# Keys of four batch pairs, then the values: reordering the projection stage of a cross-attention and dequantised-FFN kernel

## The chip, the core and the metric

The kernel runs on one core of a Trainium2 chip. The metric is the device time of one execution in microseconds (us); below, "time" means that. The engines are TensorE (PE: products and transposes; its weight loads are listed as PEld), VectorE (DVE), ScalarE (ACT), GpSimd (POOL) and SyncE (SP), whose queue issues nearly all DMAs. The engines run side by side and are held in order by semaphores alone; each executes its own list strictly in order.

## The reference

```python
# x, ctx: (8, 256, 1024) float32; 32 query heads, 8 key/value heads, head size 128
h = layernorm(x)
q = rope((h @ wq) by heads);  k = rope((ctx @ wk) by heads);  v = (ctx @ wv) by heads
x = x + softmax(q @ k.T / sqrt(128) + mask) @ v @ wo
# FFN: the row norm of a layer-normed row of 1024 is about 32, under the threshold of 64,
# so only the 4-bit table is ever picked
w = take_along_axis(lut4, the 4-bit codes of qweight)      # (1024, 1024), by bit planes
x = x + layernorm(x) @ w.T + bias
```

Every operand of a product is a float32 number split in a high part (rounded to fp32r) and a low part (the rest), and every product is made of three passes: high by high, high by low, low by high.

## The kernel before

The work has three stages. The **projection stage** makes the keys and values of all batches, writes them (high and low) to scratch memory, decodes the FFN weight, and prepares nine of the sixteen 128-row tiles of the first layer norm. The **attention stage** runs 256 units (head by batch) of queries, scores, softmax, values and output projection. The **FFN stage** is 16 row tiles by 1024 columns. The change is in the projection stage.

The projection stage goes over the batches in order (`batch(b)`, written out once for each engine). A batch has 8 key groups and 4 value groups. A key group `g` is 24 products on PE (8 chunks of the contraction by three passes, L846), with 128 columns of `wk` as the stationary operand and the 256 context columns of one batch as the moving one. Its result lies in half a PSUM bank; `k_ps` has two such places. Then ACT swaps the halves of the head into `rope_x` or `probs` (L1028, L1029), DVE multiplies the product by the cosine table (`rope_cos`, L1409), the swapped copy is multiplied by the sine table (`rope_sin`: DVE at L1418, in batch 0 POOL at L1987), DVE adds (L1424), ACT rounds to the high part (L1033), DVE subtracts for the low part (L1428) and SP stores (L581). PE may start group n when the cosine product of group n-2 is done, since that frees its bank. A value group is 24 products with 512 columns of `wv` moving (L823) into `wide_ps`; ACT rounds it, DVE subtracts (L1586), SP stores.

The context of one batch (transposed, split) lives in `ctxT`, 4096 columns of `R`. The next batch's split (ACT L1037, DVE L1433) waits until the last value group has used a chunk. `wk` fills `W` and `wv` fills `X`, split once in batch 0 (`piece_hi`, `piece_lo`, L1104 and L1544).

A layer-norm tile is loaded as rows; ACT makes mean, centre, squares and root, DVE the factor, ACT scales the row (L1069). Then PE transposes it (`turn_row`, L784, 8 products) and ACT and DVE split it (`x_high` L1082, `x_low` L1459). The seven tiles that are left for the attention stage take another way: the same statistics from rows, but the data is loaded a second time as columns (`load_columns`), the two factors come back through memory as a broadcast row, DVE adds and multiplies (L1466, L1470), ACT rounds, DVE subtracts (L1474), and nothing runs on PE.

The decoding of the FFN weight is 8 tiles of 17 DVE operations (`decode`): bit planes spread (8 small instructions, L1600), a flip (L1608), 8 leaves (L1619, 128x1024 int32) and 7 picks (L1626, COPY_PREDICATED). ACT widens bit 0 (`full_bit0`, L1162). PE transposes each decoded tile (`turn_weights`, L804) and ACT and DVE split it (L1152, L1586).

Of the kernel before, what the change touches and what calls it, by code (L numbers as in the profile page):

```python
# [14 lines left out]
def build_xattn_ffn(nc, x, ctx, mask, wq, wk, wv, wo, qweight, lut4, bias, x_rows, x_columns, rope_cos, rope_sin, out):  # L15
# [5 lines left out]
    ALU, ACT = mybir.AluOpType, mybir.ActivationFunctionType  # L21
# [23 lines left out]
    A_ROPES = NB * HKV  # L45
# [8 lines left out]
    A_TURNS = 2  # L54


    V0, V1, V2, V3, D0, D1 = range(6)
    STAGED = 6
    K_TURNS = {V1: 4, V3: 5}
    V_TURNS = {V0: 0, V2: 1, D0: 2, D1: 3}  # L60
    K_SLOT0 = HKV // 2 + len(K_TURNS)
# [3 lines left out]
    WARM = 24  # L65
    FIRST_LOADS = ((8, 9), (10,), (11, 12), (13,), (14, 15))
    FIRST_PIECES = ((3,), (4,), (5,), (6,), (7,), (8,), (9, 10), (11,))


    CARRY = {1: ((12, 13), (14,), (15,), (16,)), 2: ((15,), (16,))}  # L70
    OWN = {1: {4: 0, 5: 1, 6: 2, 7: 3}, 2: {2: 0, 3: 1, 4: 2, 5: 3, 6: 4, 7: 5}}
    LAST_OP = {0: 11, 1: 14}
    CTX_AT = {1: (2, 4), 2: (4, 7)}
# [80 lines left out]
    K_ROW = {1: 0, 2: 1, 3: 3, 4: 5, 5: 7, 6: 8}  # L154
    V_ROW = {2: 2, 3: 4, 4: 6}
    TURN_AT = [None, 5, 3] + [1] * (NB - 4)
    SECOND_AT = [None, 7, 6] + [4] * (NB - 4)
    A_ROWS = len(K_ROW) + len(V_ROW)
# [3 lines left out]
    PE_TILES = A_ROWS  # L162
# [22 lines left out]
    with ExitStack() as stack:  # L185
# [11 lines left out]
        wk_s = W[:, :].rearrange("p (c l n) -> p c l n", c=C, l=2)  # L197
        wv_s = X[:, :].rearrange("p (c l n) -> p c l n", c=C, l=2)
        ctxT = R[:, 0:4096].rearrange("p (c l n) -> p c l n", c=C, l=2)
        k_stage = R[:, 4608:5632].rearrange("p (s l n) -> p s l n", s=2, l=2)  # L200
        k_stage_all, v_stage_all = R[:, 4608:5632], R[:, 5632:6656]
# [3 lines left out]
        xT = X[:, :].rearrange("p (c l n) -> p c l n", c=C, l=2)  # L205
# [14 lines left out]
        ctx_stage = acc_t[:, 0:2048].rearrange("p (c n) -> p c n", c=C)  # L220
# [17 lines left out]
        a_raw = [raw, ln_row[:, :]] + [acc[:, t, :] for t in range(2, HT)]  # L238
        rope_x = sb("rope_x", [P, 2 * S], F32)
        rope_a = sb("rope_a", [P, 2 * S], F32)  # L240

        ropes = [(rope_x[:, 0:S], rope_a[:, 0:S]), tuple(prob_t[:, i * S:(i + 1) * S] for i in range(2))]
# [19 lines left out]
        k_ps = [bank[3][:, 0:S], bank[4][:, 0:S]]  # L262
# [10 lines left out]
        ctx_in = [sem(f"ctx_in{t}") for t in range(TS)]  # L273
# [8 lines left out]
        first_hi, first_lo = sem("first_hi"), sem("first_lo")  # L282
# [6 lines left out]
        v_stored, d_stored, first_stored = sem("v_stored"), sem("d_stored"), sem("first_stored")  # L289
        x_stored, res_stored, out_stored = sem("x_stored"), sem("res_stored"), sem("out_stored")  # L290
# [6 lines left out]
        ctx_used = sem("ctx_used")  # L297
        stage_hi, stage_lo = sem("stage_hi"), sem("stage_lo")
# [20 lines left out]
        row_ok, x_tr, x_hi, x_lo = sem("row_ok"), sem("x_tr"), sem("x_hi"), sem("x_lo")  # L319
# [4 lines left out]
        def staging(b, i):  # L324

            if b == 0 and i == D0:
                return x_split_all, first_stored
            if b == NB - 1 and i == D0:
                return prob_t[:, :].bitcast(F32R), d_stored
            keys = (V1, D1) if b == NB - 1 else (V1, V3, D1) if b == NB - 2 and i == D1 else (V1, V3)  # L330
            return (k_stage_all, k_stored[0]) if i in keys else (v_stage_all, v_stored)

        def staged_count(b, i):
            if b == NB - 1:
                return b * STAGED + (V0, V1, V2, D0, D1, V3).index(i) + 1
            return b * STAGED + i + 1

        def v_turn(b, i):

            if b == 0:  # L340
                return {V0: 0, V2: 1, D1: 2}[i]
            return b * len(V_TURNS) - 1 + V_TURNS[i]

# [24 lines left out]

        def cols_tile(e):

            return ln_row[:, :].rearrange("p (c n) -> p c n", c=C)
# [47 lines left out]
        def early_output(h):  # L419

            return (acc[:, 2, :], picks[3], picks[2], picks[1])[h]

        def a_piece(k):

            if k < HKV:
                return wk_s[:, :, :, k * DK:(k + 1) * DK]
            c, n = 2 * (k % 4), (k - HKV) // 4
            return wv_s[:, c:c + 2, :, n * BANK:(n + 1) * BANK]

        def a_source(k):  # L430
            return a_raw[k % A_SLOTS].rearrange("p (c n) -> p c n", c=C if k < HKV else 2)
# [5 lines left out]
        def _(sp):  # L437
# [10 lines left out]
            def load_row(e):  # L448

                sp.wait_ge(x_tr, 2 * min(e, PE_TILES))  # L450
                if e > PE_TILES:
                    sp.wait_ge(lo_stored, 16 * (e - PE_TILES))
                sp.dma_start(ln_row[:, :], x_tiles[e]).then_inc(row_in, 16)
# [6 lines left out]
            def load_columns(e):  # L460

                sp.wait_ge(row_step, 4 * e + 4)
                sp.dma_start(cols_tile(e), x_columns[e]).then_inc(cols_in, 16)
                sp.wait_ge(factors_out, 16 * (e - PE_TILES + 1))
                sp.wait_ge(cols_step, 2 * (e - PE_TILES))
# [7 lines left out]
            def store_high(e):  # L473

                sp.wait_ge(cols_hi, e - PE_TILES + 1)
                sp.dma_start(column_parts(e)[HI], raw.rearrange("p (c n) -> p c n", c=C)).then_inc(hi_stored, 16)
# [1600 lines left out]
```

## Time and profile before

| | |
|---|---|
| time, median of 3 runs | 2337.54 us (2337.25 to 2340.97) |
| time of the profiled execution | 2336.49 us |
| its span, first to last instruction | 2334.7 us |
| TensorE clock granted | 1.00 of full speed |
| busy: PE / DVE / ACT / POOL | 2320.7 / 1703.8 / 1108.0 / 566.1 us |
| projection stage, first key product to first query product | 7.48 to 382.76 us |
| attention stage and FFN stage | from 382.76 us, and from 2156.56 us, to the end |

The profile is one execution. A busy engine is not an engine at its peak: PE is busy 99% of the span, so a shorter time needs either less work on PE or less waiting there. Idle time of the other engines costs nothing by itself.

### The profile page before, as it was taken

What the parts mean: (1) busy time and instruction counts of PE and PEld (TensorE: products, weight loads), DVE (VectorE), ACT (ScalarE), POOL (GpSimd) and SP (SyncE); (2) the same over time, 40 slices, a digit from 0 to 9 for tenths busy, and PEclk for the clock granted to TensorE, in tenths of its full rate; (3) what the DMA queues carried; (4) which work ended last, traced back from release to release, by engine and by line L of the source; (5) the groups of instructions that cost most, each with busy time, mean ns of one, the idle gap of its engine ahead of it and who ended that gap; (6) DMA issues with size and microseconds to landing.
All of it is one profiled execution on the core that took longest, in us unless ns stands there. A gap on an engine that the chain in (4) does not pass through costs nothing.

```text
span 2334.7 us, 35083 instructions
## 1 busy us (share of the span) xinstructions
PE 2320.7 (99%) x11846; PEld 1983.3 (85%) x11846; DVE 1703.8 (73%) x3818; ACT 1108.0 (47%) x2458; POOL 566.1 (24%) x675
## 2 busy tenths in 40 slices
PE   9999999999999999999999999999999999999999
PEld 8999999888888888888888888888888888888887
DVE  8888777677777777777776777677777777777763
ACT  6555544646454646455544445444544444444110
POOL 1000001323322233223222333232223232321321
PEclk9999999999999999999999999999999999999999
DMA  7466559545454544444556643343333333334442
GB/s 268 151 205 210 191 176 313 147 135 137 126 131 118 124 135 122 127 123 135 127 163 199 205 143 109 91 118 101 116 91 113 108 100 109 98 106 163 153 135 81
DMA packets 332898, 332.85 MB, mean 143 GB/s; under 512 B 33456, under 2 KB 268080, under 8 KB 332720
## 3 DMA queue, kind: packets, MB, share of 16 engines
q1 hardware_dynamic: 297296, 314.48, 44.8%
q10 hardware_dynamic: 35424, 16.14, 2.7%
q8 instruction: 95, 1.56, 0.3%
q14 instruction: 83, 0.68, 0.1%
HBM read 186.32 MB, written 71.31 MB: 110 GB/s over the span
## 4 chain that ended last, share of the span: by engine, by line
PE 95%; DMA 2%; DVE 1%; SPq 1%; ACT 0%; issue 0%; POOL 0%; ACTq 0%; DVEq 0%
PE bank L887 29%; PE bank L959 28%; PE bank L846 8%; PE bank L997 7%; PE bank L930 7%; PE bank L903 7%; PE bank L823 7%; DMA small_split<-probs 1%; SPq L666 0%; PE bank L784 0%; PE bank L804 0%; DMA ln_row<-in_L_xattn_wk 0%; DVE residual L1861 0%; DMA small_split<-k_scratch 0%; POOL probs L2001 0%
## 5 line engine op out<-in xcount | busy, mean ns | idle before, releaser
L887 PE MATMUL bank<-acts_split,weights_split 128*128 128x512 f32 (+1 forms) x3192 | 743.0, 382 | 0.0
L959 PE MATMUL bank<-weights_split,small_split 128*128 128x512 f32 x3072 | 739.4, 389 | 3.0 <-DVE small_split L1845 1.7
L959 PEld LDWEIGHTS bank<-weights_split,small_split 128*128 128x128 f32 x3072 | 575.3, 188 | 123.4 <-DVE small_split L1845 2.9
L887 PEld LDWEIGHTS bank<-acts_split,weights_split 128*128 128x128 f32 x3192 | 576.5, 188 | 109.6
L2001 POOL TENSOR_SCALAR probs<-probs,row_numbers 128x256 f32<-128x256 f32 x512 | 355.6, 706 | 1196.7 <-DVE row_numbers L1831 1196.7
L1297 ACT ACTIVATE probs<-bank,row_numbers 128x256 f32<-128x256 f32 x512 | 237.4, 470 | 129.4 <-DVE row_numbers L1826 129.4
L1835 DVE STREAM_TRANSPOSE probs<-probs 128x512 f32<-128x512 f32 x250 | 177.6, 710 | 142.3 <-POOL probs L2001 142.3
L1993 POOL TENSOR_TENSOR rope_x<-rope_x,sin_t 128x512 f32<-128x512 f32 (+1 forms) x133 | 166.8, 1254 | 396.3 <-ACT rope_x L1270 396.3
L1840 DVE TENSOR_TENSOR small_split<-small_split 128x512 fp32r<-128x512 f32 x250 | 178.6, 714 | 94.5 <-ACT small_split L1310 94.4
L1820 DVE CUSTOM_DVE_ANT_0 bank<-bank,mask_tile 128x256 f32<-128x256 f32 x512 | 207.2, 446 | 49.3 <-PE bank L903 49.0
L903 PEld LDWEIGHTS bank<-small_split 128*128 128x128 f32 x1536 | 217.5, 190 | 21.9 <-DMA small_split<-k_scratch 1.9
L903 PE MATMUL bank<-small_split 128*128 128x256 f32 x1536 | 224.4, 282 | 0.9 <-DMA small_split<-k_scratch 0.9
L1310 ACT ACTIVATE small_split<-small_split 128x512 fp32r<-128x512 f32 x250 | 157.8, 631 | 137.3 <-DMA small_split<-probs 137.1
L1323 ACT ACTIVATE small_split<-bank 128x512 fp32r<-128x512 f32 x127 | 75.8, 597 | 303.9 <-PE bank L930 303.9
L930 PE MATMUL bank<-small_split 128*128 128x512 f32 x762 | 197.6, 394 | 3.7 <-issue 2.0
L846 PE MATMUL bank<-small_split,weights_split 128*128 128x256 f32 x1536 | 187.7, 284 | 1.3 <-issue 0.8
L846 PEld LDWEIGHTS bank<-small_split,weights_split 128*128 128x128 f32 x1536 | 185.5, 192 | 2.2 <-issue 1.2
L823 PE MATMUL bank<-acts_split,small_split 128*128 128x512 f32 x768 | 178.1, 391 | 0.1
L997 PE MATMUL bank<-weights_split,acts_split 128*128 128x512 f32 x768 | 174.5, 389 | 0.0
L997 PEld LDWEIGHTS bank<-weights_split,acts_split 128*128 128x128 f32 x768 | 144.1, 188 | 29.9
L823 PEld LDWEIGHTS bank<-acts_split,small_split 128*128 128x128 f32 x768 | 143.0, 188 | 29.5 <-DVE acts_split L1544 0.5
L1861 DVE TENSOR_TENSOR residual<-residual,bank 128x512 f32<-128x512 f32 x256 | 163.7, 681 | 0.0
(126 smaller groups left out, 2159.6 us busy)
## 6 DMA issues: line engine op xcount, KB each, us to landing
small_split<-probs SPq DMA_DIRECT2D x754, 64.0 KB, 2.2
raw<-in_L_xattn_wq SPq DMA_DIRECT2D x61, 512.0 KB, 3.7
raw<-in_L_xattn_wo SPq DMA_DIRECT2D x60, 512.0 KB, 3.9
k_scratch<-small_split SPq DMA_DIRECT2D x64, 256.0 KB, 2.4
v_scratch<-small_split SPq DMA_DIRECT2D x32, 512.0 KB, 2.9
acts_split<-x_scratch SPq DMA_DIRECT2D x32, 512.0 KB, 5.7
mask_tile<-in_mask_BxSxS_ff SPq DMA_DIRECT2D x64, 256.0 KB, 2.9
small_split<-k_scratch SPq DMA_DIRECT2D x64, 256.0 KB, 3.0
```

What stands on the lines that cost most here:

```text
L823: done = pe.matmul(wide_ps[t][:, :], ctxT[:, c, a, t * P:(t + 1) * P], wv_s[:, c, m, n * BANK:(n + 1) * BANK], start=c == 0 and k == 0, st ...
L846: done = pe.matmul(k_ps[g % 2], wk_s[:, c, a, g * DK:(g + 1) * DK], ctxT[:, c, m, :], start=c == 0 and i == 0, stop=c == C - 1 and i == 2)
L887: last = pe.matmul(query_bank(j)[:, 0:wide], wq_s[:, h, c, a, :], xT[:, c, m, b * S:b * S + wide], start=c == 0 and i == 0, stop=c == C - ...
L903: last = pe.matmul(s_ps[:, t * S:(t + 1) * S], q_s[:, Q_SLOT[u], a, t * P:(t + 1) * P], k_s[:, m, :], start=i == 0, stop=i == 2)
L930: last = pe.matmul(o_ps[:, :], v_s[:, k, a, :], pT_keys[:, m, k], start=k == 0 and i == 0, stop=k == TS - 1 and i == 2)
L959: last = pe.matmul(out_ps[part][:, :], o_s[:, a, u % 2 * S + t * P:u % 2 * S + (t + 1) * P], wo_s[:, h, m, n * BANK:(n + 1) * BANK], start ...
L997: last = pe.matmul(out_ps[f % 2 * NN + n][:, :], xT[:, c, a, f % HT * P:(f % HT + 1) * P], w4_s[:, c, m, n * BANK:(n + 1) * BANK], start=c ...
L1297: last = act.activation(row, scored, ACT.Exp, bias=neg_max[:, u % 2, t:t + 1], accum_out=row_sum[:, u % 2, t:t + 1])
L1820: last = dve.tensor_tensor_reduce(out=s_ps[:, t * S:(t + 1) * S], in0=s_ps[:, t * S:(t + 1) * S], in1=mask_t[:, t, :], scale=1.0, scalar=- ...
L1835: dve.transpose(prob_rows[:, u % 2, :], prob_rows[:, u % 2, :]).then_inc(p_blocks, 1)
L1840: dve.tensor_tensor(pT_s[:, LO, u % 2, :], source, pT_s[:, HI, u % 2, :].bitcast(F32), ALU.subtract).then_inc(pT_lo, 1)
L2001: done = pool.tensor_scalar(row, row, row_inv[:, u % 2, t:t + 1], 1.0, ALU.mult, ALU.mult)
```

## The change

- **Keys.** All key groups come first, two batches in one product: 32 groups of 24 products with 512 moving columns (`keys(j)`), each filling a whole PSUM bank. All steps of the rotation are 512 wide. The sine product is always on POOL. `ropes[1]` takes the places of `probs` and `mask_tile`.
- **Values.** Then all 32 value groups, in four segments of 8. The batch pairs come in the order 3, 0, 1, 2, so pair 3 is still in place and the others are loaded and split a second time.
- **Layout.** The split context of a pair lies in a half of `X` or `W` (8192 columns). `wv` is split at steps 24 to 31 into halves that the keys have freed. In the values part the low split of the context is on POOL.
- **Norm tiles.** The nine tiles go through columns like the other seven: `turn_row`, `x_high`, `x_low` and `row_norm` go; `load_columns`, `load_factors`, `columns_center`, `columns_scale`, `columns_high`, `columns_low`, `store_high`, `store_low` come, at fixed steps.
- **Decoding.** The order of the 136 operations is a list `DECODE`, filled step by step from a budget. Context pieces and all other side work are put at fixed steps too.
- **Start.** The first two context pieces and the first `wk` piece are split in halves; four context pieces of 512 KB are loaded for the first pair; `WARM` goes from 24 to 30.
- The attention and FFN stages keep their order; only places in `X` differ.

```diff
-    A_ROPES = NB * HKV
+    A_ROPES = NB // 2 * HKV
...
+    V_GROUPS = NB * TS * NN
+    A_STEPS = A_ROPES + V_GROUPS
+    SEGMENT = 2 * TS * NN
+    V_PAIRS = (3, 0, 1, 2)
+    CTX_PAIRS = (0, 1, 2, 3) + V_PAIRS[1:]
+    CTX_HEAD = 4
+    CTX_STEP = (3, 4, 5, 6, 10, 11, 12, 13, 18, 19, 20, 21,
+                33, 34, 35, 36, 41, 42, 43, 44, 49, 50, 51, 52)
+    PIECE_STEP = (0, 1, 2, 3, 4, 24, 25, 26, 27, 28, 29, 30, 31)
+    ROW_BASE = tuple(3 + 6 * e for e in range(9))
...
+    for step in range(5, A_STEPS):
+        spent = min(spent, 150) + 520 - (215 if step < A_ROPES else 70)
+        spent -= 125 * ((step in CTX_AT and step < A_ROPES) + (step in SPLIT_AT) + (step in QUERY_AT))
+        spent -= sum(125 for base in ROW_BASE if step in (base + 2, base + 5, base + 6, base + 7))
+        spent -= sum(150 for end in ENDED.values() if step == end + 2)
+        DECODE[step] = []
+        while n < NB * TREE and spent > 0:
+            tile, op = n // TREE, n % TREE
+            DECODE[step].append((tile, op))
+            spent -= 120 if op == 0 else 16 if op == 1 else 128 if op in (4, 7, 8, 11, 14, 15, 16) else 77
...
+    TURN_AT = {end + 2: tile for tile, end in ENDED.items()}
...
+            def keys(j):
+                pair, g = j // HKV, j % HKV
+                if j == 0:
+                    pe.wait_ge(first_lo, 3)
+                elif pair == 0:
+                    pe.wait_ge(w_lo, g + 1)
+                pe.wait_ge(rope_cosd, j + 1)
+                for c in range(C):
...
+                    for i, (a, m) in enumerate(PASSES):
+                        done = pe.matmul(k_ps[j % 2][:, :], wk_s[:, g, c, a, :], ctx_slots[pair][:, c, m, :],
+                                         start=c == 0 and i == 0, stop=c == C - 1 and i == 2)
+                done.then_inc(rope_mm, 1)
+
+            def values(v):
+                segment, b, t, n = group(v)
+                if v % SEGMENT == 0:
+                    pe.wait_ge(ctx_lo, 4 * (segment + 4))
+                if v >= 2:
+                    pe.wait_ge(val_lo, v - 1)
...
+            for step in range(A_STEPS):
+                if step < A_ROPES:
+                    keys(step)
+                else:
+                    values(step - A_ROPES)
+                if step in TURN_AT:
+                    turn_weights(TURN_AT[step])
...
+            for step in range(A_STEPS):            # VectorE
+                if step < A_ROPES:
+                    rope_cos(step)
+                ops = DECODE.get(step, ())
+                if step < A_ROPES:
+                    for tile, op in ops[:1]:
+                        decode(tile, op)
+                    ops = ops[1:]
+                    rope_add(step, step % 2)
+                else:
+                    values_low(step - A_ROPES)
...
+                for tile, op in ops:
+                    decode(tile, op)
...
+                if step < A_ROPES:
+                    rope_low(step)
...
+            for step in range(A_STEPS):            # GpSimd
+                if step < A_ROPES:
+                    turned = fold(ropes[step % 2][0], (0, 1))
+                    pool.wait_ge(rope_in, 2 + step + 1)
+                    pool.tensor_tensor(turned, turned, table(sin_t, (0, 1)), ALU.mult).then_inc(rope_sind, 1)
+                if step in CTX_AT and step >= A_ROPES:
+                    q = CTX_AT[step]
+                    pool.wait_ge(ctx_hi, q + 1)
+                    pool.tensor_tensor(ctx_piece(q)[:, :, LO, :], ctx_stage[ctx_place(q)],
+                                       ctx_piece(q)[:, :, HI, :].bitcast(F32), ALU.subtract).then_inc(ctx_lo, 1)
```

The comments "VectorE" and "GpSimd" are added here. A "step" below is one pass of this loop, 0 to 63: one group on PE and the side work that belongs to it.

## Rows read from the trace of the kernel before

**Rows 1.** The page: its head line, and busy time by engine.
```profile
span 2334.7 us, 35083 instructions
...
PE 2320.7 (99%) x11846; PEld 1983.3 (85%) x11846; DVE 1703.8 (73%) x3818; ACT 1108.0 (47%) x2458; POOL 566.1 (24%) x675
```

**Rows 2.** Groups by line and form on PE: count, busy us, mean ns, idle before.
```profile
L846 PE MATMUL bank<-small_split,weights_split 128*128 128x256 f32 x1536 | 187.7, 284 | 1.3 <-issue 0.8 <-DVE weights_split L1544 0.5
L823 PE MATMUL bank<-acts_split,small_split 128*128 128x512 f32 x768 | 178.1, 391 | 0.1
...
L784 PE MATMUL bank<-ident,ln_row 128*128 128x128 f32 x72 | 9.3, 272 | 0.0
```

**Rows 3.** The chain that ended last: start us, length us, engine and line.
```profile
77.81 5.47 PE bank L823 x24
84.15 16.34 PE bank L823 x72
100.49 11.51 PE bank L846 x96
112.88 11.51 PE bank L846 x96
...
382.76 10.88 PE bank L887 x48
```

**Rows 4.** Timeline of the start: start us, length us, engine, line, what.
```profile
6.03 1.15 ACT L1108 ACTIVATE weights_split<-raw 128x512 fp32r<-128x512 f32 x2 [1.02 <-DMA raw<-in_L_xattn_wk]
...
7.48 3.36 PE L846 MATMUL bank<-small_split,weights_split 128*128 128x256 f32 x24 [0.82 <-issue]
7.67 1.15 ACT L1037 ACTIVATE small_split<-residual 128x512 fp32r<-128x512 f32 x2 [0.50 <-DMA residual<-in_ctx]
...
10.27 1.06 ACT L1104 ACTIVATE weights_split<-residual 128x1024 fp32r<-128x1024 f32 x1 [0.27 <-DMA residual<-in_L_xattn_wk]
...
11.30 20.42 PE L846 MATMUL bank<-small_split,weights_split 128*128 128x256 f32 x168 [0.46 <-DVE weights_split L1544]
```

**Rows 5.** Timeline, DVE and POOL side by side, in three places.
```profile
15.38 0.74 POOL L1987 TENSOR_TENSOR probs<-probs,sin_t 128x256 f32<-128x256 f32 x1 [2.20 <-ACT probs L1029]
...
15.78 0.63 DVE L1428 TENSOR_TENSOR small_split<-rope_a,small_split 128x256 fp32r<-128x256 f32 x1
...
445.16 1.21 DVE L1551 TENSOR_TENSOR weights_split<-raw,weights_split 128x1024 fp32r<-128x1024 f32 x1
445.34 1.83 POOL L2001 TENSOR_SCALAR probs<-probs,row_numbers 128x256 f32<-128x256 f32 x2 [7.68 <-DVE row_numbers L1831]
...
465.25 0.93 POOL L2001 TENSOR_SCALAR probs<-probs,row_numbers 128x256 f32<-128x256 f32 x2 [3.80 <-DVE row_numbers L1831]
```

**Rows 6.** Groups by line and form on DVE, 0 to 383 us.
```profile
L1626 DVE COPY_PREDICATED residual<-residual 128x1024 f32<-128x1024 uint8 x56 | 75.4, 1346 | 0.7
L1619 DVE TENSOR_SCALAR residual<-residual,probs 128x1024 int32<-128x1024 int32 x64 | 50.8, 818 | 1.1 <-ACT residual L1162 1.1
...
L1428 DVE TENSOR_TENSOR small_split<-probs,small_split 128x256 fp32r<-128x256 f32 x32 | 14.2, 442 | 0.1
```

**Rows 7.** Groups by line and form on POOL, whole span.
```profile
L1993 POOL TENSOR_TENSOR rope_x<-rope_x,sin_t 128x512 f32<-128x512 f32 x123 | 159.4, 1296 | 395.4 <-ACT rope_x L1270 395.4
L2015 POOL TENSOR_TENSOR residual<-residual,probs 128x1024 f32<-128x1024 f32 x16 | 38.3, 2399 | 112.6 <-DVE ln_row L1516 101.0 <-DMA probs<-in_L_ffn_bias 11.6
```

**Rows 8.** Groups by line and form on DVE, 383 to 2150 us.
```profile
L1796 DVE TENSOR_TENSOR rope_a<-rope_a,rope_x 128x512 f32<-128x512 f32 x123 | 85.1, 692 | 34.3 <-POOL rope_x L1993 31.5
```

**Rows 9.** Timeline, a stretch of decoding on DVE.
```profile
344.60 1.54 DVE L1619 TENSOR_SCALAR residual<-residual,probs 128x1024 int32<-128x1024 int32 x2 [1.05 <-ACT residual L1162]
...
346.17 1.32 DVE L1626 COPY_PREDICATED residual<-residual 128x1024 f32<-128x1024 uint8 x1
...
347.39 0.80 DVE L1619 TENSOR_SCALAR residual<-residual,probs 128x1024 int32<-128x1024 int32 x1
```

**Rows 10.** Groups by line and form on ACT, 0 to 383 us.
```profile
L1162 ACT ACTIVATE residual<-residual 128x1024 int32<-128x1024 uint8 x8 | 8.4, 1051 | 5.0 <-DVE probs L1608 3.1 <-DVE residual L1600 1.8
```

More of the change, by code:

```diff
@@ L261, in build_xattn_ffn @@
         w4_ps = [bank[0], bank[1]]
-        k_ps = [bank[3][:, 0:S], bank[4][:, 0:S]]
+        k_ps = [bank[3], bank[4]]
         q_ps = [bank[3], bank[4]]
@@ new lines, in _ @@
+            for tick in range(2, A_STEPS + 1):
+                if 0 <= tick - 2 < A_ROPES:
+                    store_keys(tick - 2)
+                if tick in CTX_AT:
+                    load_context(CTX_AT[tick])
+                if tick in ROW_STEP:
+                    if tick == ROW_BASE[0]:
+                        sp.wait_ge(ctx_lo, CTX_HEAD)
+                    load_row(ROW_STEP[tick])
+                if tick + 1 in SPLIT_AT and SPLIT_AT[tick + 1] >= HKV:
+                    load_split(SPLIT_AT[tick + 1])
+                for tile in range(1, NB):
+                    if tick == BEGUN[tile - 1] + 2:
+                        load_planes(tile)
+                    if tick == LUT_FREE[tile - 1] + 2:
+                        load_lut(tile)
+                if tick == A_STEPS - 10:
+                    sp.wait_ge(ctx_lo, 4 * len(CTX_PAIRS))
@@ new lines, in _ @@
+                if tick > A_ROPES:
+                    store_values(tick - A_ROPES - 1)
+                if tick - 3 in ROW_STEP:
+                    store_factors(ROW_STEP[tick - 3])
+                    load_columns(ROW_STEP[tick - 3])
+                if tick - 4 in ROW_STEP:
+                    load_factors(ROW_STEP[tick - 4])
+                if tick - 8 in ROW_STEP:
+                    store_high(ROW_STEP[tick - 8])
+                    store_low(ROW_STEP[tick - 8])
+                if tick - 1 in TURN_AT:
+                    for i in range(2):
+                        store_weights(TURN_AT[tick - 1], i)
@@ new lines, in values @@
+            def values(v):
[4 more added lines that the diff above has]
+                    pe.wait_ge(val_lo, v - 1)
+                first = b % 2 * S + t * P
+                for c in range(C):
+                    if v in (0, SEGMENT // 2) and c % 2 == 0:
+                        pe.wait_ge(w_lo, HKV + n * 4 + c // 2 + 1)
+                    for i, (a, m) in enumerate(PASSES):
+                        done = pe.matmul(wide_ps[v % 2][:, :], v_ctx[segment][:, c, a, first:first + P], wv_s[n][:, c, m, :],
+                                         start=c == 0 and i == 0, stop=c == C - 1 and i == 2)
+                done.then_inc(wide_mm, 1)
@@ L1303, in turned_high @@
                 act.wait_ge(o_mm, 1 + u // 2)
+                if u == 1:
+                    for s in range(2):
+                        act.wait_ge(v_stored[s], 16 + 8 * V_GROUPS)
                 if u in PE_TURNS:
@@ L1633, in decode @@
             def decode(tile, op):
-                A, B, C_, D_ = range(4)
+                A, B, C_, D_ = roles(tile)
                 if op == 0:
```

918 lines of the change are left out of this document (341 added, 577 removed).

## The prediction

> **What bounds the kernel now.** I read the page first: PE is busy 2320.7 of 2334.7 us [rows 1], so the end moves only if PE has less to do or waits more. Next the groups on PE: the key groups of the projection stage (L846) waited 1.3 us in all, the value groups 0.1 us [rows 2]. Then the chain of waits for lengths from start to start: a value group is 5.47 us for 24 products, a key group 11.51 / 4 = 2.88 us for 24 products of half the width [rows 3]. A busy mean of one product is no price, since products overlap. From the first key product (7.48 us) to the first query product (382.76 us) PE hardly ever stops [rows 3, 4]. So the change must be read in this stage, first as PE work, then as whether the helpers, mostly DVE, still keep up.
>
> The sum is made against the profiled execution, 2336.49 us (span 2334.7, some 1.8 us around it). That is 1.05 us under the median of the runs; I add that at the end.
>
> **Keys, two batches per product.** 64 groups of 2.88 us (184.3) go. 32 groups of 512 columns come. The trace has no such key group, but the value groups have the same form, 24 products of 128x512, at 5.47 us, and 48 query products take 10.88, the same to 1% [rows 3]: 32 x 5.47 = 175.0. Saving 9.3 us. Bounds: at the query price 32 x 5.44 = 174.1; if two narrow groups were no slower than a wide one, nothing.
>
> The Trainium skill ("TensorE: Matmul & The Clock Gate", Back-to-back issue gap) puts a lone warm product at N / 2.4 ns plus 2.5 ns, by which the 24 narrow ones would take 2.62 us and the wide ones 5.18, and the merge would save 1.9 us and not 9.3. The rows, 2.88 and 5.47, disagree with it for products that alternate with weight loads, so the rows decide.
>
> **Row tiles off PE.** Between two value groups lies a transposed tile: 84.15 - 77.81 - 5.47 = 0.87 us [rows 3]. There are 72 / 8 = 9 [rows 2]: 7.8 us go. Nothing is put in their place on PE. The weight turns stay: 112.88 - 100.49 - 11.51 = 0.88 each [rows 3], eight of them.
>
> **Start.** Before, the first key product began at 7.48; the second group began at 11.30, so the stage ran as if begun at 11.30 - 2.88 = 8.42 [rows 4]. The first pair needs the first and third transfers as context, the second as `wk`. They arrived so that ACT began at 6.03 (second) and 7.67 (third) [rows 4]. With halves (ACT 0.6, DVE 0.7 each) the third's first half is done at about 9.0, and keys start there, 1.5 us later than before. Chunks 4 to 7 need the fourth and fifth transfers; ACT began on the fifth at 10.27 [rows 4]. Behind six ACT halves and two whole pieces, DVE ends the last at about 13.0, while PE would be there at 9.0 + 2.7 = 11.8. So the first group ends near 15.7, as if begun at 10.3. Cost +1.9 us. The six extra warming transposes lie in the wait for the loads, so cost nothing; without that cover they are 6 x 0.2.
>
> **PE alone.** The stage would end at 10.3 + 64 x 5.47 + 8 x 0.88 = 367.4 in place of 382.76: **-15.4 us**, execution 2321.1.
>
> **Do the helpers keep up?** This is where I expect the gain to shrink. I price DVE from start to start, since its instructions overlap by some 0.1 us: 0.6 for 512 wide (0.69 long [rows 8]), 1.13 for 1024 two-source (1.21 long [rows 5]), 1.57 for two leaves (346.17 - 344.60), 1.22 for a pick (347.39 - 346.17), up to 1.35 where a pick follows a pick [rows 6, 9].
>
> POOL's part grows. Before, it had 8 sine products of 256 wide and was then idle until the queries. Now it has 32 of 512 at 1.29 us and 12 low splits of 1024; the nearest row of that shape takes 2.40 us [rows 7]. Does this cost DVE anything? The timeline says yes. While POOL multiplied from 15.38 to 16.12, DVE's two-source subtraction of 15.78 took 0.63, and 0.44 is its mean [rows 5, 6]. At 445.34 POOL's pair took 1.83, against 0.93 when alone at 465.25, and ended 0.80 after DVE's two-source instruction (to 446.37) did [rows 5]. That is one after the other, released about 0.14 before the end of each record. So a POOL instruction keeps a two-source DVE instruction out for its length less 0.14: 1.15 and 2.26 us. Sources in PSUM (cosine product, value and weight lows) go through.
>
> The Trainium skill ("SBUF — State Buffer", Who interferes with whom) says the same of two-source instructions and adds one-source instructions in a two-port mode, the leaves by their speed. The trace agrees for the former; no row shows the decoding beside POOL.
>
> Sums over steps, by the `DECODE` list:
> - Steps 5 to 31: rotation 27 x 1.8 = 48.6, decoding 35.1, context splits 11.3, `wv` splits 9.0, norm tiles 4.7 + 13.6 (twelve column operations), weight lows 2.4. DVE 124.6, POOL 27 x 1.15 = 31.0, together 155.6. PE has 27 x 5.47 + 2 x 0.88 = 149.4. Excess 6.2.
> - Steps 32 to 60: decoding 94.3, value lows 17.4, columns 16.9, the rest 10.9. DVE 139.5, POOL 27.1, together 166.6, against PE's 163.0. Excess 3.6. Besides, ACT waits for DVE's bit planes in order to widen bit 0, 1.05 us [rows 10], and rounds the next value group (0.58) only behind that. With DVE late it then has nothing to do for 1.6 to 1.8 us, in five tiles: +9.
>
> Total excess 18.8. Off it: PE needs a bank again one step later, so DVE may lag by 5.47 - 0.62 - 0.69 = 4.2 us before PE notices; and in the quarter of the key steps in which DVE isn't late, the cosine product lies beside POOL's instruction, 7 x 0.6 = 4. What reaches PE: 18.8 - 4.2 - 4 = **10.6 us**. Bounds: nothing, if the decoding isn't kept out (then DVE has 124.6 for 149.4 and 139.5 for 163.0); and 19, if neither credit holds.
>
> **Other parts.** ACT loses 18 half-tile roundings and 9 scalings and gains 9 roundings of columns and 12 context pieces; its steps come to at most 6.3 us and about 2.8 on average, so it has room. Column loads, factor stores and broadcasts (3 to 5 us to land) are issued by SP one to three steps ahead; behind SP's wait for the factor (L457) stands the next key store, which is not due before that either. The second loading of 12 context pieces adds 6 MB to a stage that moves 80. The first query needs its `wq` split, made from step 60 on, and context and turned rows, loaded from tick 56 on, 4 to 8 steps ahead. All this I cost at nothing; a load that comes a step late costs up to 5 us once. The other stages have the same work and order: 0.
>
> **Sum.** 2336.5 - 15.4 + 10.6 = 2331.7 on the profiled execution; with 1.05, **2332.5 us**.
>
> **The rivals.**
> 1. *The cover holds.* Decoding isn't blocked by POOL, or DVE's gaps take it all up. For: PE's wait on DVE in this stage is 0.5 us now [rows 2]. Against: rows 5, and sums of 1.02 and 1.04 of PE's time. 2321.1 + 1.05 = 2322.
> 2. *Slower: DVE and POOL become the bound of the stage.* The same mechanism, with neither credit: late instructions never lie beside POOL's, and each wait of ACT for DVE empties DVE's list. 2321.1 + 19 + 1.05 = 2341. The change turns slower than before once more than 15.4 us of PE waits arise, that is when excess less lag passes 15.4. For: the steps with most decoding (42 to 44, 49 to 52) are just those with POOL's long splits. Against: sums near 1.0 let small gaps be used.
> 3. *No gain from width.* A wide key group costs two narrow ones, 5.76: +9.3, so 2341.8. Against it: rows 3 have 5.47 for the form. By the skill's gap it would be 7.4 us worse than I sum; that is this rival in its mild form.
> 4. *The clock falls at the start.* PE waits 1.1 to 1.5 us at 8 and 12 us. The granted clock stayed at its upper level, 2.4 GHz, through the present waits of 0.82 and 0.46 us [rows 4]. At half of it a key group takes 5.5 us more: 2338.
>
> **How the numbers follow.** Forecast 0.52, rival 1 0.25, rival 2 0.17, rivals 3 and 4 0.03 each. A difference of 0.2% (4.7 us) is about what a measurement can tell from none. Faster by more is under 2332.8: all of rival 1 and half the forecast's cases, 0.51. Within: 0.37, from the forecast's other half and part of rivals 2 to 4. Slower, over 2342.2: 0.12. The range goes from rival 1 less 2 us for the price of a wide group, 2320, to rival 2 and a little more, 2342.5. The forecast's own range is 2326 to 2338.
>
> **What the profile would show.** Right: the key line with 768 products of 128x512, 5.47 us per 24; no line for turned rows; the query stage beginning at about 378 us; PE waiting about 10 us on DVE, for the cosine product late in the keys part and for value lows around steps 44 to 55; DVE's two-source instructions and picks beside POOL stretched to 2 us. If it begins near 367 with picks at their 1.3, rival 1 is right; if at 385 or later, rival 2. Wrong throughout if another stage changes its length, or if PE waits for a DMA or for ACT.

## The result, and the profile after

The changed kernel takes 2362.72 us (median of 4 runs, 2358.81 to 2366.27), the kernel before 2337.39 on the same chip: 1.0108 of it, 95% interval 1.0095 to 1.012. I had forecast 2332.5 in a range of 2320 to 2342.5. The sign was wrong, and the time lies 20 us beyond the range.

The page of the profiled execution (2358.81 us, the fastest of the four and 3.9 under their median; 1.8 of it lie around the span), against [rows 1]:

```profile
span 2357.0 us, 33040 instructions
...
PE 2317.0 (98%) x11012; PEld 1940.6 (82%) x11012; DVE 1725.4 (73%) x3661; ACT 1095.3 (46%) x2342; POOL 638.9 (27%) x711
```

PE is busy 3.7 us less and the span is 22.3 longer. The chain says where: the first query product, at 382.76 before [rows 3], begins at 405.60. That is 22.8, so the projection stage holds all of it, and the rest is as long as before.

```profile
13.16 19.31 PE bank L853 x84
...
372.02 27.22 PE bank L869 x120
400.11 5.48 PE bank L869 x24
405.60 10.88 PE bank L898 x48
```

A wide group takes 27.22 / 5 = 5.44 us, as forecast, and groups of turned rows are gone. The groups on PE from 0 to 406 us (count | busy us, mean ns | idle before), against [rows 2]:

```profile
L853 PE MATMUL bank<-acts_split,weights_split 128*128 128x512 f32 x768 | 180.4, 396 | 10.5 <-DVE rope_a L1349 7.6 <-DVE acts_split L1498 2.1 <-DVE acts_split L1366 0.8
L869 PE MATMUL bank<-weights_split,acts_split 128*128 128x512 f32 x192 | 47.0, 404 | 7.5 <-DVE small_split L1523 7.5
L869 PE MATMUL bank<-weights_split 128*128 128x512 f32 x192 | 46.7, 402 | 4.9 <-DVE small_split L1523 4.9
L869 PE MATMUL bank<-acts_split 128*128 128x512 f32 x192 | 45.9, 400 | 2.3 <-DVE small_split L1523 2.3
L869 PE MATMUL bank<-acts_split,weights_split 128*128 128x512 f32 x192 | 44.5, 391 | 1.7 <-DVE small_split L1523 1.7
L832 PE MATMUL bank<-ident,residual 128*128 128x128 f32 x64 | 8.4, 274 | 1.6 <-DVE residual L1567 1.6
```

L853 are the key groups, L869 the value groups (by their operands' buffers), L832 the weight turns. 28.5 us of waits where before had 1.4, every one of them ended by DVE. 2.9 lie at the start and were in the sum. PE's own work would have ended the stage at 367.4. 38.2 us are lost, 25.6 of them in waits. The other 12.6 are slower groups, and the windows (columns: stretch, its length, then busy us of PE, PEld, DVE, ACT, POOL, granted clock, DMA share, GB/s) show why for most of them:

```profile
115.00:120.00 5.00, 5.00 (x17) 3.93 (x16) 4.64 (x8) 2.77 (x8) 1.29 (x1) 0.67 0.76 221
...
140.00:145.00 5.00, 3.00 (x7) 2.38 (x8) 5.00 (x6) 1.53 (x3) 0.79 (x1) 0.72 0.58 161
...
335.00:340.00 5.00, 3.79 (x10) 2.99 (x11) 4.43 (x4) 4.97 (x8) 3.07 (x1) 0.67 0.43 142
```

After some of the waits, here of 1.84, 4.79 and 2.48 us, the granted clock is at its lower level (1.2 GHz of 2.4) for part of the stretch. Over the eight windows of 5 us that show it, 8.4 us of full clock are missing. The rest is a group's start after a wait, 5.7 us where a group in a row takes 5.45.

**What DVE waited for.** A list that is too long for its engine leaves the engine no idle time. But DVE was busy 331.2 of the 406 us (309.2 of 383 before), and it had idle time in front of just the instructions that PE then waited for (L1349 is the cosine product, L1523 the value low; 0 to 406 us):

```profile
L1349 DVE TENSOR_TENSOR mask_tile<-bank,cos_t 128x512 f32<-128x512 f32 x16 | 11.0, 690 | 6.4 <-ACT probs L1040 6.4
L1349 DVE TENSOR_TENSOR rope_a<-bank,cos_t 128x512 f32<-128x512 f32 x16 | 11.0, 688 | 13.8 <-ACT rope_x L1040 13.8
...
L1523 DVE TENSOR_TENSOR small_split<-bank,small_split 128x512 fp32r<-128x512 f32 x31 | 21.4, 690 | 20.1 <-ACT small_split L1142 20.1
```

Some of this is plain waiting for PE's group. But ACT waited itself, and much of it for transfers:

```profile
L1142 ACT ACTIVATE small_split<-bank 128x512 fp32r<-128x512 f32 x32 | 19.0, 594 | 66.1 <-DMA v_scratch<-small_split 36.0 <-PE bank L869 25.4 <-DMA k_scratch<-small_split 4.7
L1049 ACT ACTIVATE acts_split<-residual 128x1024 fp32r<-128x1024 f32 x16 | 16.9, 1058 | 25.4 <-DMA residual<-in_ctx 25.2
```

L1142 rounds a value group, L1049 a context piece. One step of the latter kind in the timeline (L544 is SP's context load, L1133 the rounding of the keys, L1366 DVE's context low):

```profile
87.84 0.47 SPq L544 DMA_DIRECT2D residual<-in_ctx  x1
...
94.07 0.67 DVE L1356 TENSOR_TENSOR mask_tile<-mask_tile,probs 128x512 f32<-128x512 f32 x1
95.83 1.06 ACT L1049 ACTIVATE acts_split<-residual 128x1024 fp32r<-128x1024 f32 x1 [4.56 <-DMA residual<-in_ctx]
96.80 0.61 ACT L1133 ACTIVATE small_split<-mask_tile 128x512 fp32r<-128x512 f32 x1
96.93 1.22 DVE L1366 TENSOR_TENSOR acts_split<-residual,acts_split 128x1024 fp32r<-128x1024 f32 x1 [2.18 <-ACT acts_split L1049]
...
98.74 0.69 DVE L1349 TENSOR_TENSOR rope_a<-bank,cos_t 128x512 f32<-128x512 f32 x1
```

The context piece was issued at 87.84 and took 8 us to arrive. ACT stood for it 4.56 us with the rounding of the keys queued behind, DVE then stood 2.18, and the next cosine product came late. PE had slack there and waited only 0.53. The longest wait of PE in the stage, 4.79 us until 142.00, has the same shape. These are pieces of the chain ahead of it:

```profile
125.50 10.65 DMA residual<-in_ctx
...
136.18 1.07 ACT acts_split L1049
...
137.27 1.22 DVE acts_split L1366
```

The median landings of the stage, after and then before:

```profile
v_scratch<-small_split SPq DMA_DIRECT2D x31, 512.0 KB, 6.0
residual<-in_ctx SPq DMA_DIRECT2D x26, 512.0 KB, 5.6
w_scratch<-small_split SPq DMA_DIRECT2D x16, 512.0 KB, 6.2
```

```profile
v_scratch<-small_split SPq DMA_DIRECT2D x31, 512.0 KB, 2.9
residual<-in_ctx SPq DMA_DIRECT2D x16, 512.0 KB, 4.2
w_scratch<-small_split SPq DMA_DIRECT2D x14, 512.0 KB, 3.7
```

**POOL and the decoding.** The row I lacked is there now, the decoding (L1560 leaves, L1567 picks) beside POOL's low splits:

```profile
222.71 2.40 POOL L1859 TENSOR_TENSOR weights_split<-residual,weights_split 128x1024 fp32r<-128x1024 f32 x1 [2.21 <-ACT weights_split L1049]
222.74 3.64 DVE L1560 TENSOR_SCALAR residual<-residual,probs 128x1024 int32<-128x1024 int32 x2
...
227.05 3.32 POOL L1859 TENSOR_TENSOR weights_split<-residual,weights_split 128x1024 fp32r<-128x1024 f32 x1 [1.94 <-ACT weights_split L1049]
228.04 3.53 DVE L1567 COPY_PREDICATED residual<-residual 128x1024 f32<-128x1024 uint8 x1
```

Two leaves take 3.64 in place of 1.54 [rows 9], a pick 3.53 in place of 1.35: both are kept out. For the leaves the Trainium skill ("SBUF — State Buffer", Who interferes with whom) says this of one-source instructions in a two-port mode, and the trace agrees; it does not name the pick. But over the stage it comes to less than I charged. Picks rose from 1346 [rows 6] to 1553 ns, leaves from 818 to 947:

```profile
L1567 DVE COPY_PREDICATED residual<-residual 128x1024 f32<-128x1024 uint8 x56 | 87.0, 1553 | 1.0
L1560 DVE TENSOR_SCALAR residual<-residual,probs 128x1024 int32<-128x1024 int32 x64 | 58.6, 947 | 0.5
```

56 x 0.207 + 64 x 0.129 = 19.8 us, and with the key lows (mean 823 and 749 against some 684), the column operations and the table's XOR some 30. I had charged 31.0 + 27.1 = 58.1. That POOL makes these 30 us is shown by the kernel without POOL below (`e3_pool_idle`): picks take 1336 ns there, leaves 818, the key lows 685 and 683.

### The profile page after: what moved, and what is told of

The parts are those of the page before. It is cut to its first block, busy times and chain, and to the rows that moved or that the text cites. A ratio compares the mean times of both kernels' runs of the same rounds, so it can differ in the third digit from the quotient of the medians.

```text
span 2357.0 us, 33040 instructions
## 1 busy us (share of the span) xinstructions
PE 2317.0 (98%) x11012; PEld 1940.6 (82%) x11012; DVE 1725.4 (73%) x3661; ACT 1095.3 (46%) x2342; POOL 638.9 (27%) x711
## 4 chain that ended last, share of the span: by engine, by line
PE 81%; DVE 9%; DMA 4%; ACT 2%; issue 2%; SPq 1%; POOL 1%; ACTq 0%; DVEq 0%
PE bank L898 28%; PE bank L970 28%; PE bank L1008 7%; PE bank L914 7%; PE bank L940 7%; DVE residual L1567 2%; PE bank L869 2%; DVE residual L1560 1%; DMA small_split<-probs 1%; DMA residual<-in_ctx 1%; PE bank L853 1%; DMA v_scratch<-small_split 1%; POOL probs L1874 0%; DVE raw L1393 0%; DVE residual L1726 0%
## 5 line engine op out<-in xcount | busy, mean ns | idle before, releaser
L898 PEld LDWEIGHTS bank<-acts_split,weights_split 128*128 128x128 f32 x3192 | 576.5, 188 | 109.6
L914 PEld LDWEIGHTS bank<-small_split 128*128 128x128 f32 x1536 | 217.7, 190 | 20.5 <-DMA small_split<-k_scratch 0.5
L853 PE MATMUL bank<-acts_split,weights_split 128*128 128x512 f32 x768 | 180.4, 396 | 10.5 <-DVE rope_a L1349 7.6
L853 PEld LDWEIGHTS bank<-acts_split,weights_split 128*128 128x128 f32 x768 | 145.5, 191 | 44.4 <-DVE rope_a L1349 9.7
L940 PEld LDWEIGHTS bank<-small_split 128*128 128x128 f32 x762 | 134.9, 189 | 28.3 <-issue 3.2
L1215 ACT ACTIVATE small_split<-rope_a 128x512 fp32r<-128x512 f32 (+1 forms) x133 | 81.9, 615 | 152.4 <-DVE rope_a L1661 147.8
```

The costliest lines, as they stand in the source:

```text
L853: done = pe.matmul(k_ps[j % 2][:, :], wk_s[:, g, c, a, :], ctx_slots[pair][:, c, m, :], start=c == 0 and i == 0, stop=c == C - 1 and i == 2)
L898: last = pe.matmul(query_bank(j)[:, 0:wide], wq_s[:, h, c, a, :], xT[b // 2][:, c, m, b % 2 * S:b % 2 * S + wide], start=c == 0 and i == 0 ...
L914: last = pe.matmul(s_ps[:, t * S:(t + 1) * S], q_s[:, Q_SLOT[u], a, t * P:(t + 1) * P], k_s[:, m, :], start=i == 0, stop=i == 2)
L940: last = pe.matmul(o_ps[:, :], v_s[:, k, a, :], pT_keys[:, m, k], start=k == 0 and i == 0, stop=k == TS - 1 and i == 2)
```

## The experiments

Three theories. **A**: POOL keeps DVE out (the forecast's mechanism). **B**: transfers come late, by SP's order and by their own landing, and ACT, DVE and PE hand the delay on. **C**: DVE simply has too much to do. Times are medians; "stage end" is the first query product of the profiled execution (382.60 before, 405.44 after, in the timeline).

**1. Who does POOL's work?** In the first, DVE's condition becomes `if step in CTX_AT:` and POOL's branch goes; in the second the sine product goes to DVE:

```diff
                 if step < A_ROPES:
                     rope_cos(step)
+                    rope_sin(step)        # the same product, on DVE
```

> The twelve low splits of context pieces in the values part go from POOL to DVE; all else is as in the changed kernel (2362.7 us). Theory A (POOL's instructions keep DVE's decoding and two-source instructions out): twelve times 2.3 us of lockout become twelve times 1.13 us of DVE's own work, so PE's waits for value lows (16.5 us) fall by about 10: 2350 to 2356 us. Theory B (what is late are transfers and SP's ordered queue, DVE is only their last link): DVE gets 13.6 us more work and nothing else changes: 2361 to 2370.

> The 32 sine products of the keys part go from POOL to DVE. Theory A: 1.15 us of lockout becomes some 0.6 us of DVE's own work, 32 times, so PE's waits for the cosine product (7.6 us and what follows in half clock) go mostly: 2350 to 2358. Theory B: DVE has 19 us more work and the late transfers stay: 2361 to 2372.

> Both of the former: POOL does nothing in the projection stage. Theory A: 38.2 us of lost PE time fall to some 12 to 20: 2336 to 2346. Theory B: 2360 to 2375, DVE being no freer for it.

Measured: 2361.76 (interval of the ratio to before 1.0093 to 1.0123), 2371.91 (1.0136 to 1.0179) and 2364.11 (1.0101 to 1.0134). At my prices theory A fails: without POOL the stage ends at 405.58. Taking the sine from POOL even costs 9 us. At my price (1.15 us of lockout, 0.69 of DVE's own time) it should have given 14.7. The profile of the first kernel, in which POOL has only the sine products, says why: picks, leaves, key lows and the XOR take some 12 us longer than with POOL idle, for 32 products that I had charged 36.8, and on DVE they are 21.8 us of work. So POOL's sine products were a help. Presumably most of them fall where DVE waits or reads PSUM; no view counts that.

These edits don't show that the lockout was harmless. The third takes some 30 us of stretching from DVE and gives it some 37 us of work (21.8 for the sine, 14.8 for the splits). No run took POOL's work away without giving it to DVE. By the rate that experiment 4 finds, 0.25 to 0.36 us per us of DVE time, my estimate for the 30 us is 7 to 11 us of the loss.

**2. Less for DVE.**

```diff
-                decoding[tile].mark(dve.tensor_scalar(picks[dst].bitcast(I32), bit0, ...
+                decoding[tile].mark(dve.tensor_scalar(picks[dst].bitcast(I32)[:, 0:512], bit0[:, 0:512], ...
```

and the pick likewise on `[:, 0:4]` of its eight bit groups. Half of the decoded weights are then not computed.

> Leaves and picks of the weight decoding work on half of the columns, so half of the decoded weights are not computed; POOL does what it did, all transfers stay. DVE has some 55 us less to do in the stage. Theory A in its wide form (DVE with its lockouts is the bound): PE waits go to under 8 us, 2328 to 2336. Theory B: PE still waits where a store or a load is late, 20 us or more of waits: 2345 to 2360.

Measured: 2341.57, stage end 383.01, between the two theories. 21 us go, some 20 of the 41 over PE's own 2322 stay, and the chain of that kernel runs through transfers:

```profile
121.28 11.09 DMA residual<-in_ctx
...
330.05 10.07 DMA v_scratch<-small_split
```

By the stage end 22.4 us go. So DVE's load matters and it isn't all.

**3. One late transfer at a time.**

```diff
-                if tick - 3 in ROW_STEP:         # first: store_factors, load_columns; all behind it one later
+                if tick - 4 in ROW_STEP:
-    CTX_STEP = (3, 4, 5, 6, 10, 11, 12, 13, 18, 19, 20, 21, 33, 34, 35, 36, 41, ...
+    CTX_STEP = (3, 4, 5, 6, 8, 10, 12, 14, 16, 18, 20, 22, 33, 34, 36, 38, 41, ...     # second
-        v_stage = (R[:, 4608:5632], R[:, 5632:6656])
+        v_stage = (R[:, 4608:5632], R[:, 5632:6656], R[:, 1024:2048])                  # third, for keys too
```

> SP takes the store of a norm tile's factors, the load of its columns and the broadcast back one step later in its order, and everything behind them (centre, scale, round, store) one step later too. SP now waits 27.7 us for factors and 24.3 us for the landing of their store, with key stores and context loads behind it. Theory B (SP's order and late transfers): those 52 us of SP waiting go to under 15 and PE waits shrink by 3 to 10 us: 2353 to 2360. Theory C (DVE alone has too much work): DVE does the same instructions, 2361 to 2365.

> Context pieces are split every second step where four in a row stood (8, 10, 12, 14 for 10 to 13, and so on), and each is loaded one step before it is split, where its place is free by then. Theory B: ACT's waits for context landings (38.7 us in the changed kernel's stage) fall below 12, PE's waits for cosine products and context parts with them: 2350 to 2357. Theory C: unchanged within 3 us, 2360 to 2366.

> A third staging place for the split keys and values (in 4 KB that nothing uses in this stage), so a store may take one step longer to land before ACT waits for it. Theory B: ACT's 36 us of waits for value stores and 10 for key stores fall below 10, PE's 16.5 us on value lows fall by half or more: 2350 to 2357. Theory C: 2360 to 2365.

> The three edits together. Theory B: what is left is DVE's excess of some 10 us as forecast, 2333 to 2345. Theory C: 2358 to 2366.

Measured: 2369.04, 2366.62, 2363.85, and 2358.29 for all three (1.0077 to 1.0107). Singly none helps the time; together they give 4 us, far from the 20 that theory B asked for. In the profiled executions the stage ends at 401.39, 404.73, 405.68 and 399.49. So the first did end the stage 4.1 us earlier, but its profiled execution then took 1967.8 us to the end where the changed kernel took 1951.6. This happens in all experiments to some degree (see the last section), so stage ends are given beside the times from here on. The profile of the fourth shows what still stood in the way:

```profile
200.11 0.37 SPq L615 DMA_DIRECT2D k_scratch<-small_split  x1
...
205.06 0.60 ACT L1144 ACTIVATE small_split<-bank 128x512 fp32r<-128x512 f32 x1 [7.50 <-DMA k_scratch<-small_split]
205.69 0.69 DVE L1527 TENSOR_TENSOR small_split<-bank,small_split 128x512 fp32r<-128x512 f32 x1 [5.62 <-ACT small_split L1144]
...
206.44 2.07 PE L871 MATMUL bank<-acts_split 128*128 128x512 f32 x4 [3.70 <-DVE small_split L1527]
```

The first value group is rounded into the place of a key store that has only just been issued. Two more of the kind: a decoding table that took 8 us to land, and value stores behind the loads of the turned rows.

**4. All transfers ahead, and then less for DVE.** Value part `v` goes to place `(v + 2) % 3`; planes and tables get second places (`prob_t[:, 512:656]`) and are loaded a tile ahead; one chunk of turned rows per step; mask and first keys at step 40.

> On top of the three edits: value parts begin in the staging place whose key store is oldest, bit planes and tables have a second place each and are loaded a tile ahead, the turned rows for the queries are loaded one chunk per step over eight steps where two per step stood in four, and the first mask and keys are loaded 15 steps earlier. In the kernel with the three edits ACT still waited 10.7 us for value stores and 8.7 for key stores, DVE 6.7 for a table, and three PE waits of 3.35 to 6.45 us had such a transfer ahead of them. Theory B: those waits go, PE's waits fall by 10 to 15 with the clock's share: 2340 to 2349. Theory C (DVE's work is the bound whatever the transfers do): 2354 to 2360.

> The former with leaves and picks on half of the columns (half of the decoded weights are not computed). If late transfers and DVE's load are the only two causes, nothing of the 38 us is left but the start: 2321 to 2327. If a third cause exists (the clock, PE's own price per group), it stays above 2332.

> The first of these with centre, scale and low part of the nine norm tiles on one of eight column blocks (the other seven are left uncomputed); all transfers and ACT's rounding stay. DVE has 9 x 3 x 1.0 = 27 us less. If the column path's DVE work is what overfills DVE, this gives what half the decoding gives, per us of work: 8 to 12 us under the first. If it lies in steps where DVE has room: 0 to 4.

Measured: 2348.91 (1.0034 to 1.007), 2336.46 and 2339.96; stage ends 385.84, 374.10, 377.28. With experiment 3 the transfers account for 13.8 us of the time and for 19.6 of the stage, as theory B in its full form. The other two leave out half of the decoded weights, and seven of eight column blocks of the nine norm tiles. Half the decoding gives 12.4 more for 49 us less of DVE work, the column operations 8.9 for 25 (I had reckoned with 27): 0.25 and 0.36 us per us of work. So B and C both hold. 2336.46 is 10 over my bound, though: partly a wait of 2.6 us, and half clock after it, at the first query, whose rows I now loaded too late, and partly time behind the stage. In the profile of the first, theory A's mechanism shows where the transfers no longer cover it. A column low takes 2.59 us where 1.22 is its length with POOL idle, and an XOR of 128x8 takes 2.35 where it takes 0.16 alone. What the wait of PE behind them owes to them is not separated:

```profile
258.86 5.75 POOL L1864 TENSOR_TENSOR acts_split<-residual,acts_split 128x1024 fp32r<-128x1024 f32 x2 [19.97 <-ACT acts_split L1051]
...
259.77 2.59 DVE L1405 TENSOR_TENSOR raw<-raw,small_split 128x1024 fp32r<-128x1024 f32 x1 [1.08 <-ACT small_split L1085]
...
262.28 2.35 DVE L1553 TENSOR_TENSOR probs<-probs 128x8 int32<-128x8 int32 x1
...
267.70 1.53 PE L871 MATMUL bank<-weights_split 128*128 128x512 f32 x5 [3.33 <-DVE small_split L1527]
```

**5. The order between DVE, ACT and POOL.** The first loads the turned rows over six steps. The second is the first with experiment 1's first edit. The third is the first with the bit planes at the start of a step and ACT's widening right behind its value rounding; the fourth has both. The edit for the planes:

```diff
             tile, op = n // TREE, n % TREE
+            if op == 0 and DECODE[step]:
+                break
...
+                    if ops and ops[0][1] == 0:
+                        decode(*ops[0])
+                        ops = ops[1:]
                     values_low(step - A_ROPES)
```

> The kernel with all transfers ahead (2348.9 us), but the turned rows for the first query are loaded over six steps and not eight. In the runs with less DVE work the first query waited 2.6 to 3.1 us for their last chunk and went on at half clock, some 4 us in all; in the kernel itself 0.65. Theory D (that wait was made by the slower loading): it goes; 2345 to 2349 here. Otherwise it stays at 2349 or, the bunching being back, 2352.

> The former with the twelve low splits of the values part on DVE. Done alone in the changed kernel, this moved the time by 1 us. Theory A' (POOL's 2.4 us splits do keep DVE out for more than DVE's own 1.13, but late transfers hid it): 4 to 10 us under the former. Theory A'' (lockout and own work cost DVE the same): within 3 us.

> The first of these with the bit planes spread at the beginning of a step, ahead of the value low, and ACT's widening right behind its value rounding, so ACT's rounding of the next value group no longer waits for DVE's last instruction of a step. DVE now waits 1.61 us in each of five tiles for that rounding. If that chain counts: 3 to 8 us under the first. If DVE is so full that the wait is only moved: within 3.

> Both edits on the first. If both count, 2333 to 2340, about the kernel before; if neither, 2345 to 2349.

Measured: 2350.95, 2348.79, 2348.51 and 2342.71 (1.0015 to 1.0039). The first edit is worth nothing by itself. Each of the two others gives some 2 us alone, less than runs of one kernel differ by (the first ran from 2347.18 to 2356.55), and both together 8.2. The stage ends, 390.57, 389.43, 387.85 and 383.89, go the same way: 1.1 and 2.7 alone, 6.7 together. Against the kernel of experiment 4 (2348.91, 385.84) the fourth gains 6.2 us of time and 2.0 of the stage. That freeing one of two things that a step waits for leaves the other would fit this; it isn't shown.

**6. What is left.** The order of the turned-row loads alone, and the kernel with both edits and little DVE work:

```diff
-                    for c in ((0, 1), (2, 3), (4,), (5,), (6,), (7,))[tick - A_STEPS + 8]:
+                    for c in ((0,), (1,), (2,), (3,), (4, 5), (6, 7))[tick - A_STEPS + 8]:
```

> The kernel with both edits (2342.7 us), the turned rows loaded one chunk per step over eight steps. In its profile one wait of 4.39 us was left at 359 us, behind a value store that took over 5 us to land while all 16 queues were busy with two chunks per step. If that bunching makes the wait: it goes with its half clock (6 us), and the first query waits 1 to 3 us for the last chunk instead: 2338 to 2342. If not: 2342 to 2345.

> The same, with one chunk per step for four steps and then two steps of two, so the last chunk comes two steps earlier than with one per step. If both waits are made by the order of these loads, neither is there: 2335 to 2339, the kernel before's time. If the bunched steps only move the wait to 380: 2340 to 2344.

> The kernel with both edits, and leaves and picks on half of the columns, and centre, scale and low part of the nine norm tiles on one column block of eight (the rest of both is not computed): DVE has some 75 us less. PE's own work is that of the change. If the forecast's PE terms hold (-9.3 for the keys, -7.8 for the turned rows, +1.9 for the start), nothing else is left and it takes 2321 to 2326; a dearer wide key group or a dearer start would show as 2330 or more.

Measured: 2342.08, 2342.86 and 2329.07. The loads' order changes nothing; the wait at 359 us stays with 3.2 and 3.1 us. The kernel that it was read from (the fourth of experiment 5) has it with 4.39 us, and its chain there runs through the store and the broadcast of a norm tile's factors:

```profile
339.46 7.46 DMA factor_scratch<-row_numbers
...
346.93 8.09 DMA column_factors<-factor_scratch
```

```profile
355.12 1.22 DVE L1401 TENSOR_TENSOR raw<-raw,column_factors 128x1024 f32<-128x1024 f32 x1 [5.76 <-DMA column_factors<-factor_scratch]
...
358.77 0.68 DVE L1531 TENSOR_TENSOR small_split<-bank,small_split 128x512 fp32r<-128x512 f32 x1
```

ACT had rounded the value group by 354.63. DVE stood before a column operation for its factors, did two picks, and only then made the low part that PE waited for. The two kernels here have the same chain, with DVE standing 4.07 and 3.75 us. So this wait belongs to the norm tiles' way through memory and not to the turned rows. In the same stretch SP's issue of a weight store stood 7.14 us at 351.16. No run moved these factors alone in this kernel.

The last kernel leaves out both kinds of DVE work that experiment 4 left out, and settles PE's own terms. Its timeline on PE:

```profile
13.93 90.02 PE L856 MATMUL bank<-acts_split,weights_split 128*128 128x512 f32 x396 [1.55 <-DVE acts_split L1374]
...
104.57 65.55 PE L856 MATMUL bank<-acts_split,weights_split 128*128 128x512 f32 x288
...
345.14 16.62 PE L872 MATMUL bank<-acts_split,weights_split 128*128 128x512 f32 x72 [0.93 <-DVE small_split L1534]
...
367.96 11.04 PE L901 MATMUL bank<-acts_split,weights_split 128*128 128x512 f32 x48
```

With 0.93 us of waits behind the start the queries begin at 367.96, where the forecast had 367.4 for PE alone.

## Why the prediction was wrong, by its own steps

- **Keys 64 x 2.88 to 32 x 5.47**: right. Groups take 5.44 to 5.45.
- **Row tiles off PE** and **Start +1.9**: right. The last kernel's stage end leaves 0.6 us for all PE terms together. The second half of the first group began at 13.16, forecast 13.0. The clock did not fall at the start, so rival 4 is out, but it fell in the middle of the stage, where I had no term for it: up to 8.4 us.
- **"Do the helpers keep up?"**, 10.6 us: this step failed. 38.2 were lost. Not because POOL or DVE took longer than priced; the lockout was half of what I charged. It failed by its form. I added up each engine's work over 28 steps, set it against PE's time, and allowed a lag of 4.2 us. DVE was then busy 328 us between the first key product and the first query product, 92% of the 357 that PE alone was to take (87% in the keys part, 97% in the values part). That leaves little room for waits *of* DVE, and the sum had none. DVE waited 20.2 us before cosine products, 20.1 before value lows and 8.7 before context lows, all for ACT. The keys part lost 12 us (first value product at 199.26, PE alone 187.1) and the values part 26.
- **"Other parts ... all this I cost at nothing"**: this step failed too, and it is where DVE's waits come from. I had checked that transfers are issued one to three steps ahead, with the landings of the kernel before. The stage moves 93.75 MB at a share of 74% where it moved 80.07 at 63%, and a value store lands in 6.0 us in place of 2.9. Value stores and ACT's rounding share two places, so 10.9 us for a group, its rounding, its low and the landing became tight. Taking the transfers' lateness away gave 13.8 us of the time, 19.6 of the stage. "ACT has room" was true of its sum and not of its order: one late context piece holds the rounding of the keys behind it.
- **ACT waiting on bit planes**, 9 us: a real chain. Undone together with POOL's splits it gave 8.2 (6.7 by the stage end), alone 2.4 (2.7).
- **The rivals**: rival 2 had the right sign and the right engines at the end of the chain, and its turning point (15.4 us of waits) was passed; its price, 19, was half. No rival had the transfers in it. I had named "if PE waits for a DMA or for ACT" as what would prove me wrong, and PE never did so directly: each wait was ended by DVE, which had itself waited. Rival 3's 2341.8 was summed wrongly besides: it adds 9.3 to the forecast with the helpers' 10.6 kept whole, but slower key groups give the helpers that time too.

The account by times: 2362.7 to 2348.9 by transfers, to 2342.7 by the order of bit planes and splits, to 2329.1 by less DVE work. By stage ends: 405.44 to 385.84, to 383.89, to 367.96. So within the stage transfers were worth 19.6 us and the load of DVE 15.9, and the order at most a few. The last 7 us to the 2322 of PE alone lie behind the stage. No version with the whole computation beats the kernel before: the best is 2342.1 (1.0011 to 1.0028 of it). Of the 15.4 us gained on PE, 7.8 come from the nine norm tiles. They put 27 column operations on DVE (35.9 us with their stretching) in place of 18 low parts (12.5 us), and leaving most of the 27 out gave 8.9. So by that run this half of the change gains about nothing. No run kept these tiles on PE beside the wide key groups.

## What to carry to other kernels

Once an engine's list comes near the time that it must keep (here 92% of it over the stage, 97% in its second part), a sum of work no longer prices the stage: go through the steps in order with every in-order queue, and ask of each instruction what it stands behind. A transfer's landing time belongs to the traffic around it; price a change that adds traffic with longer landings, above all where a store must land before its place is written again. And where several things are late together, undoing one may show nothing: undo all, and then put one back. Where runs of one kernel differ by more than the effect, read the end of the changed stage beside the time.

## What the runs showed that I had not expected

- A `COPY_PREDICATED` of 128x1024 beside a 2.4 us POOL instruction takes 3.53 us in place of 1.35, and POOL's own instruction then grows to 3.3 to 3.5: they hold each other up.
- SP's issue of one 512 KB store took 7.14 us, in a stretch (351 to 358 us) in which the 16 DMA engines had no idle time (the DMA share reads 1.04), and the next issue in SP's order came at 358.34.
- From the first query product to the end, the profiled execution took 1952.1 us before and 1951.6 after, but 1954.7 to 1971.5 in the experiments, with the same work. The highest figure overstates it: that execution (half the decoding, transfers ahead) was the slowest of eleven, 10.9 over their median. In the last kernel, whose profile lies 1.1 over its median, it is 1960.3. The larger figures come with up to 13 us of PE idle before L942, put down to "issue" and DVE. This takes back part of what they gained. I can't say what makes it.
